# Sparse attention with a top-64 cut: GpSimd hides the found scores, VectorE counts the narrow tile, and the maxima move to the next step

## The reference

```python
q, k, v = split_heads(x @ Wq), split_heads(x @ Wk), split_heads(x @ Wv)   # x: 16 batches, 512 rows, 128 columns
k = concat([mem_k, k]); v = concat([mem_v, v])                # 16 memory keys before 512, 16 heads of 64
dots = einsum('bhid,bhjd->bhij', q, k) * 64 ** -0.5
dots = einsum('bhij,hk->bkij', dots, pre_proj)                # mix the heads
dots = where(causal, -FMAX, dots)
vk = top_k(dots, 64)[..., -1:]                                # each row's 64th largest score
dots = where(dots < vk, -FMAX, dots)
attn = einsum('bhij,hk->bkij', softmax(dots), post_proj)      # mix again
out = einsum('bhij,bhjd->bhid', attn, v) @ Wo + bo            # then a residual, layer norms and a gated FFN of 384
```

## Time and profile before

| | before |
|---|---|
| median of 3 runs | 3637.55 us (3636.05 to 3637.64) |
| the profiled execution | 3636.07 us, span 3634.3 us |
| VectorE busy | 3292.4 us, 91% |
| ScalarE busy | 3199.3 us, 88% |
| PE busy | 2795.9 us, 77% |
| GpSimd busy | 1551.4 us, 43% |

### The profile page before, as it was taken

How to read it: one execution, slowest core, us unless ns; L and a number is a source line. 1 busy time by engine, 2 the same in 40 slices (tenths; PEclk the granted TensorE clock), 3 DMA queues, 4 the chain that set the end, 5 groups by cost and what they waited for, 6 DMA issues and landing times. The chain is left out here.

```text
span 3634.3 us, 67348 instructions
## 1 busy us (share of the span) xinstructions
PE 2795.9 (77%) x13751; PEld 1808.7 (50%) x13751; DVE 3292.4 (91%) x12492; ACT 3199.3 (88%) x9018; POOL 1551.4 (43%) x2663
## 2 busy tenths in 40 slices
PE   7777778777777878778778867877777788877765
PEld 3455455545545545555455545544555455545544
DVE  4699999999999999999999999999999999999994
ACT  1799999999979999999999979998999999999973
POOL 3233444444434444444444444443444444444433
PEclk9888999988888899888998888899889998899886
DMA  1000000000000000000000000000000000000000
GB/s 41 7 2 2 5 8 5 8 2 5 8 4 8 5 8 2 5 8 5 8 5 7 2 4 8 5 8 2 5 8 5 8 5 8 2 5 8 2 7 4
DMA packets 31375, 22.37 MB, mean 6 GB/s; under 512 B 3201, under 2 KB 30338, under 8 KB 30722
## 3 DMA queue, kind: packets, MB, share of 16 engines
q1 hardware_dynamic: 30722, 16.03, 1.6%
HBM read 11.83 MB, written 4.19 MB: 4 GB/s over the span
## 5 line engine op out<-in xcount | busy, mean ns | idle before, releaser
L871 ACT ACTIVATE signs<-scores,state 128x528 int8<-128x528 f32 (+3 forms) x3072 | 1764.3, 574 | 181.8 <-DVE state L1149 103.4
L713 PE MATMUL s_bank<-xn,gT 128*128 128x512 f32 (+3 forms) x2048 | 900.6, 568 | 1.7 <-issue 0.7
L1269 POOL TENSOR_SCALAR probs<-probs,rinv 128x528 f32<-128x528 f32 (+3 forms) x1024 | 547.1, 553 | 507.3 <-DVE rinv L1053 507.3
L737 PE MATMUL t_bank<-ident,probs 128*128 128x128 f32 x2560 | 482.7, 313 | 299.1 <-POOL probs L1269 289.7
L724 PEld LDWEIGHTS y_bank<-u_all,probsT 128*128 128x128 f32 x5120 | 619.9, 194 | 133.4 <-issue 124.2
L724 PE MATMUL y_bank<-u_all,probsT 128*128 128x128 f32 x5120 | 625.2, 278 | 7.1 <-ACT probsT L882 7.1
L1260 POOL TENSOR_TENSOR offset<-consts,found 128x36 f32<-128x36 f32 x256 | 161.7, 632 | 1047.5 <-DVE work L1014 1047.5
L871 ACT ACTIVATION_READ_ACCUMULATOR signs<-scores,state 128x1 f32 x3072 | 575.7, 187 | 0.0
L737 PEld LDWEIGHTS t_bank<-ident,probs 128*128 128x128 f32 x2560 | 299.7, 153 | 506.8 <-issue 398.6
L1048 DVE SCALAR_TENSOR_TENSOR probs<-scores,kth,expo 128x528 f32<-128x528 f32 (+3 forms) x1024 | 522.8, 565 | 24.8 <-issue 19.1
L892 ACT ACTIVATE expo<-scores,negmax 128x528 f32<-128x528 f32 (+3 forms) x1024 | 535.0, 575 | 0.0
(11 more groups left out here) (148 smaller groups left out, 3384.9 us busy)
## 6 DMA issues: line engine op xcount, KB each, us to landing
xwork<-in_L_attn_x_dram SPq DMA_DIRECT2D x17, 256.0 KB, 2.8
xres<-in_L_attn_x_dram SPq DMA_DIRECT2D x16, 256.0 KB, 2.9
out_dram<-ybuf SPq DMA_DIRECT2D x16, 256.0 KB, 2.4
u_all<-in_L_attn_Wq_dram SPq DMA_DIRECT2D x1, 512.0 KB, 3.7
u_all<-in_L_attn_Wk_dram SPq DMA_DIRECT2D x1, 512.0 KB, 4.5
u_all<-in_L_attn_Wv_dram SPq DMA_DIRECT2D x1, 512.0 KB, 5.3
u_all<-in_L_attn_Wo_dram SPq DMA_DIRECT2D x1, 512.0 KB
expo<-in_L_ffn_w_gate_dram SPq DMA_DIRECT2D x1, 192.0 KB, 4.7
```

The source lines that it names most:

```text
L713: nc.tensor.matmul(score_part(t, 0, KEYS[t]), lhsT=gT[s % 2][:, t * P:(t + 1) * P], rhs=xn[par][:, 0:KEYS[t]], start=True, stop=False, ski ...
L737: mm = nc.tensor.transpose(t_bank[q % 2][:, at:at + P], probs[:, h % 2, KEY_AT[t] + j * P:KEY_AT[t] + (j + 1) * P], ident[:, :])
L871: nc.scalar.activation(signs[:, k, 0:ROW[t]], row(scores, ring(head_of(s, k + 1), RING), t), ACT.Sign, bias=guesses(s % STATES, k, GUESSES ...
L1269: nc.gpsimd.tensor_scalar(prb, prb, rinv[:, slot_p, t:t + 1], 1.0, ALU.mult, ALU.mult).then_inc(scaled, 1)
```

## The change

Four things are changed in a step.

1. The hiding leaves VectorE. POOL does `work = scores - work` in four instructions, one for each tile, after its scaling, and posts `hidden`. For a subtraction of 1 to hide a score, all scores are made tiny: a factor `UNIT = 2 ** -60` goes into `a_all` and `amem`, and is taken out again in the exponentials' scale and in `minus_unit`.
2. The maxima and the pick move from the end of a step to the beginning of the next one, and wait for `hidden`.
3. Of the four founds, two stay ahead of `probs` and two come behind `rinv`.
4. ScalarE counts three tiles for each guess, not four. The 144-wide tile is counted by VectorE (`marks`, `narrow`), three instructions a step, and one more small instruction merges them.

Beside these, POOL places the memory scores before it scales, PE makes all three turns before the flag's product, some of the extra products move by a step, and the FFN's and the last norm's VectorE and POOL work moves one step later. The number of transfers is the same.

```diff
-                        for p, t in enumerate(ORDER):
-                            at_least(act, counted[k], 4 * (g - k - 1) + p)
+                        for p, t in enumerate(ORDER[:3]):
+                            at_least(act, counted[k], 3 * (g - k - 1) + p)
                             nc.scalar.activation(signs[:, k, 0:ROW[t]], ...
...
+                    if applies:                                       # VectorE, first in the step
+                        dve.wait_ge(hidden, 4 * gp + 4)
+                        for p, t in enumerate(ORDER):
+                            v.max(candidates(past)[:, t, 1:9], work[:, AT[t]:AT[t] + ROW[t]]).then_inc(select_step, 1)
+                        dve.wait_ge(offset_ready, gp + 1)
...
                     if selects:
-                        count_found(ORDER[0])
-                        count_found(ORDER[1])
+                        for t in ORDER[:2]:
+                            count_found(t)
...
                         v.reciprocal(rinv[:, slot_p % 2, :], rowsum[:, :]).then_inc(rinv_ready, 1)
+                    if selects:
+                        for t in ORDER[2:]:
+                            count_found(t)
...
-                        v.scalar_tensor_tensor(out=work[:, :], in0=work[:, :], scalar=-FMAX,
-                                               in1=scores[:, bass.ds(slot_k, 1), :].squeeze(1),
-                                               op0=ALU.mult, op1=ALU.add).then_inc(select_step, 1)
...
+                        for k in counts_now:
+                            v.tensor_scalar(marks[:, k], row(scores, ring(head_of(s, k + 1), RING), 0),
+                                            guesses(now, k, GUESSES)[:, 0:1], None, ALU.is_ge, ALU.add,
+                                            accum_out=narrow[:, k:k + 1]).then_inc(narrow_step, 1)
...
+                        dve.wait_ge(narrow_step, len(counts_now))
+                        dve.sem_clear(narrow_step)
+                        v.scalar_tensor_tensor(out=narrow_miss, in0=narrow[:, :], scalar=-2.0, in1=narrow_aim,
+                                               op0=ALU.mult, op1=ALU.add).then_inc(guess_step, 1)
+                        v.tensor_tensor(wide_miss, wide_counts, wide_aim, ALU.subtract).then_inc(guess_step, 1)
...
+                        for p, t in enumerate(ORDER):                 # POOL, behind its scaling
+                            pool.wait_ge(found_ready, 4 * gk + p + 1)
+                            alone(pool)
+                            wrk = work[:, AT[t]:AT[t] + ROW[t]]
+                            nc.gpsimd.tensor_tensor(wrk, row(scores, slot_k, t), wrk, ALU.subtract).then_inc(hidden, 1)
```

More of the change, by code:

```diff
@@ L418, in build @@
         found_ready = sem("found_ready")
+        hidden = sem("hidden")
         offset_ready = sem("offset_ready")
+        narrow_step = sem("narrow_step")
         select_step = sem("select_step")
@@ L755, in step @@
                     if lagged(kind, s, LAG_P):
-                        turn(head_of(s, LAG_P), g - LAG_P, 0)
-                        turn(head_of(s, LAG_P), g - LAG_P, 1)
+                        for q in range(3):
+                            turn(head_of(s, LAG_P), g - LAG_P, q)
                     if flagged(kind, s):
@@ L1071, in step @@
                         norm_stats(kind, b, "X1", xres)
-                    if s == 14 and kind != "first":
+                    if 11 <= s < 11 + HC and kind != "first":
+                        c = s - 11
+                        dve.wait_ge(silu_pool, HC * (b - 1) + c + 1)
+                        v.scalar_tensor_tensor(out=f_up[:, c, :], in0=f_tanh[:, c, :], scalar=1.0,
+                                               in1=f_up[:, c, :], op0=ALU.add, op1=ALU.mult).then_inc(silu_ready, 1)
+                    if s == 15 and kind != "first":
@@ L1088, in top_scan @@
[L1088 to L1101, removed]
@@ L1255, in step @@
                         nc.gpsimd.tensor_copy(seed_place((s + 1) % STATES), seed[:, s, :, :]).then_inc(first_ready, 1)
-                    if lagged(kind, s, LAG_K):
-                        at_least(pool, kth_ready, g - LAG_K)
-                        pool.wait_ge(found_ready, 4 * (g - LAG_K) + 4)
-                        alone(pool)
-                        nc.gpsimd.tensor_tensor(offset[:, :, 0:9], ranks, found[:, :].unsqueeze(2).to_broadcast([P, T, 9]),
-                                                ALU.add).then_inc(offset_ready, 1)
-                    if lagged(kind, s, LAG_P):
-                        gp, slot_p = g - LAG_P, head_of(s, LAG_P) % 2
-                        pool.wait_ge(rinv_ready, gp + 1)
-                        at_least(pool, probs_ready, 4 * gp + 4)
-                        alone(pool)
-                        for t in SCORE_ORDER:
-                            prb = probs[:, slot_p, AT[t]:AT[t] + ROW[t]]
-                            nc.gpsimd.tensor_scalar(prb, prb, rinv[:, slot_p, t:t + 1], 1.0, ALU.mult,
-                                                    ALU.mult).then_inc(scaled, 1)
-                        if s == LAG_P and kind != "first":
-                            pool.wait_ge(misc_full, misc_index(kind, b, ("PM", 1)) + 1)
-                        pool.wait_ge(scaled, 4 * gp + 4)
-                        alone(pool)
-                        nc.gpsimd.tensor_copy(head_mem(pmem, head_of(s, LAG_P)), mem_parts(probs[:, slot_p, :])).then_inc(pmem_ready, 1)
                     if kind != "drain":
@@ L1286, in step @@
                                               head_mem(smem[par], s)).then_inc(mem_placed, 1)
+                    gp, slot_p = g - LAG_P, head_of(s, LAG_P) % 2
+                    if lagged(kind, s, LAG_P):
+                        pool.wait_ge(rinv_ready, gp + 1)
+                        at_least(pool, probs_ready, 4 * gp + 4)
+                        alone(pool)
+                        for t in SCORE_ORDER:
+                            prb = probs[:, slot_p, AT[t]:AT[t] + ROW[t]]
+                            nc.gpsimd.tensor_scalar(prb, prb, rinv[:, slot_p, t:t + 1], 1.0, ALU.mult,
+                                                    ALU.mult).then_inc(scaled, 1)
+                    if lagged(kind, s, LAG_K):
+                        gk, slot_k = g - LAG_K, ring(head_of(s, LAG_K), RING)
+                        for p, t in enumerate(ORDER):
+                            pool.wait_ge(found_ready, 4 * gk + p + 1)
+                            alone(pool)
+                            wrk = work[:, AT[t]:AT[t] + ROW[t]]
+                            nc.gpsimd.tensor_tensor(wrk, row(scores, slot_k, t), wrk, ALU.subtract).then_inc(hidden, 1)
+                        at_least(pool, kth_ready, gk)
+                        alone(pool)
+                        nc.gpsimd.tensor_tensor(offset[:, :, 0:9], ranks, found[:, :].unsqueeze(2).to_broadcast([P, T, 9]),
+                                                ALU.add).then_inc(offset_ready, 1)
+                    if lagged(kind, s, LAG_P):
+                        if s == LAG_P and kind != "first":
+                            pool.wait_ge(misc_full, misc_index(kind, b, ("PM", 1)) + 1)
+                        pool.wait_ge(scaled, 4 * gp + 4)
+                        alone(pool)
+                        nc.gpsimd.tensor_copy(head_mem(pmem, head_of(s, LAG_P)), mem_parts(probs[:, slot_p, :])).then_inc(pmem_ready, 1)
                     extras(kind, b, s)
```

150 lines of the change are left out of this document (79 added, 71 removed).

## The result

The change makes the kernel 8.8% slower: 3958.84 us median against 3637.6, ratio 1.0883 with a 95% interval of 1.0864 to 1.0902. The profiled execution's span is 3957.3 us, 323 more than before.

The account below looks back on a forecast made before the run. VectorE's list was taken as the bound. Hides holding its two-input instructions add 1.45 us a step: 256 x 1.45 = 371, + 12 = 383; 3636 + 383 = 4019, say 4020 us, 10.5% slower; range 3860 to 4120.

Parts of the forecast that it names:

- The bound: Whole kernel: VectorE's list sets the time, 12.29 us a plain step without gaps; ScalarE's time buys at most about 20 us.
- The split of the founds and the moved maxima cost the same as before: VectorE's step: these pieces only change places, and the flag's load stays between long instructions; no added time.
- VectorE's list with nothing held: VectorE's plain step after the change, if POOL held nothing: 11.78 us instead of 12.29.
- POOL's hides: POOL's four subtractions behind the scaling: 1.30, 1.02, 0.75 and 0.48 us, 3.55 in all, ending 6.04 us after rinv.
- The collision: After rinv, hides hold spread, missed and the merging instruction; update ends at 7.99 us, step 13.74 instead of 12.29, +1.45.
- The small POOL work: Offset, pmem and negmax on POOL behind the hides: counted as costing nothing, at most 0.7 us a step.
- The 12 us for the 48 steps: Steps s = 6, 7 and 14: spread was not held before, so 0.25 us isn't saved; 48 x 0.25 = 12 us.
- The sum: Whole run: 256 steps x 1.45 = 371, + 12 = 383 us more than 3636.
- the hides hold nothing: Rival: hides don't hold VectorE, so the chain rinv, scaling, hides, maxima, probs bounds at 11.9 us; 3548 us, chance 0.12.
- The narrow counts: Forecast: one-input counts run beside the hides. Rival: they are held too, step 14.75 us, 4278 us in all, chance 0.05.
- The hides' rate: POOL's hides: forecast 2.14 ns a column. Rival: a broadcast subtraction's 1.68 ns, step 13.27 us, 3899 us, chance 0.11.
- the sum hardly depends on the order: VectorE's small instructions beside the hides: whichever comes first, the update can't be over much before the hides are.

Follow-up runs that it names:

- Run 1: The changed kernel with POOL's four hides working on one column each and the maxima reading the unhidden scores: 3513.61 us, 0.9671 of before.
- run 5: The changed kernel with the narrow counts placed ahead of spread and missed: 3849.16 us, 1.0582 of before.
- run 2: The changed kernel with ScalarE counting all four tiles again, no narrow counts on VectorE: 3798.55 us, 1.0453 of before.
- run 7: The changed kernel with hiding back on VectorE, all counts on ScalarE, and the flag's load two founds later, behind the first found: 3675.12 us, 1.0101 of before.
- run 10: The changed kernel with hiding on VectorE, all counts on ScalarE, f_up early in the next step, flag's load behind the fourth maxima: 3510.77 us, 0.9658.
- run 6: The kernel before, with two of the four founds behind rinv, which also put the flag's load behind the first found: 3702.49 us, 1.0178 of before.

## Why the prediction was right

It forecast 4020 us in 3860 to 4120; 3958.8 was measured. By its steps:

- *The bound.* VectorE's list sets the time before and after; ScalarE's 378 us bought nothing. Right. But the step read as typical, 12.29 us, was not. It follows the memory maxima, and VectorE has no gap in it. The next step has one, between its last found and its first probs, 0.40 us from start to start instead of 0.28 (1487.37 to 1487.65 in the earlier trace rows):

```profile
1499.66 0.36 DVE L1014 TENSOR_SCALAR_CACHE_REDUCE work<-scores,state 128x144 f32<-128x144 f32 x1
...
1500.06 0.77 DVE L1048 SCALAR_TENSOR_TENSOR probs<-scores,kth,expo 128x528 f32<-128x528 f32 x1
```

  The gap is over 0.05 us in 170 steps. In the change, where the flag's load stands among the maxima, it is gone from the usual step. So "The split of the founds and the moved maxima cost the same as before" is wrong by 0.12 us a plain step, about 30 us of what the forecast was too high by.
- *VectorE's list with nothing held*, 11.78 us. Run 1 shows it: rinv to rinv is 11.76 us in its plain steps (median).
- *POOL's hides*: forecast 1.30, 1.02, 0.75, 0.48, measured 1.304, 1.029, 0.762, 0.489. They overlap a little, so that they end 5.91 us behind rinv, not 6.04. POOL is busy 470 us more, 1.84 a step, where the forecast has 3.6 - 1.2 = 2.4: it left out that the offset no longer waits either (671 ns before, 247 after).
- *The collision.* From the maxima to rinv 5.75 us, as forecast. From rinv to the maxima 7.80 instead of 7.99. The merging instruction comes at 5.75, not 5.96, since the founds follow rinv after 0.10 instead of 0.14, and missed is released at 4.7 instead of 4.8. It takes 171 ns, against 166 in run 1, and with the update behind it 2.05 us instead of 1.95. 0.19 x 256 = 49 us is the larger part of what was too much.
- *The small POOL work*, which the forecast let cost nothing. It costs: the update's next two instructions fall on the offset and the pmem copy. The first of them in the change, then in run 1:

```profile
L1152 DVE TENSOR_TENSOR state<-counts,consts x258: 153/283/1315, 115.1 to 3885.4; 128x9 f32<-128x9 f32 x129
...
L1152 DVE TENSOR_TENSOR state<-counts,consts x258: 152/160/174, 112.5 to 3440.3; 128x9 f32<-128x9 f32 x129
```

  The second (L1153) goes from 176 ns in run 1 to 267. (Before, the update has eleven instructions, not ten, from L1123 to L1149; in the change it has twelve from L1150 on.) From the merging instruction to the maxima it is 2.05 us in the change and 1.85 in run 1, so that 0.2 us a step is what it costs, within the 0.7 named as the most. The forecast's 1.95 with nothing held was 0.1 too long and covered half of it.
- *The 12 us for the 48 steps* in which spread was not held before: there. From start to start, spread takes 1.10 us more than before at s = 6, 7 and 14 and 0.80 on average in the others, 0.30 x 48 = 14 us. The other steps lost 31 us over the plain step's loss in all, 19 more than these 12; the forecast saw no difference there.
- *The sum.* Forecast 371 + 12 = 383 us; the spans differ by 323. The plain step is 79 us too high (292 instead of 371: 49 by the half step from rinv, 30 by the 12.29), the other steps 19 too low (31 instead of 12). The errors partly cancel, so the time is nearer than its terms.
- *The rivals.* That the hides hold nothing falls with run 1, which is the same list with hides of one column. The narrow counts are not held: 352 ns at the median with 362 at most, while they run beside the hides. The hides' rate is that of f_up and not of the broadcast subtraction.
- *The sentence that the sum hardly depends on the order* holds in the plain step (run 5) and not in the steps with one-input work to spare, where order is worth 2 us (16.07 against 13.96 at s = 6).

That the hides hold VectorE's two-input instructions is shown by run 1, and that one-input work beside them is not held by the counts and by L966 in run 2; which part of the two engines is shared is not seen in any run.

## What to carry to other kernels

Work moved from VectorE to GpSimd is not off VectorE's path if it is long and VectorE has small two-input instructions at that time: each of these can wait for the end of a whole GpSimd instruction (1.1 us here for four columns). Look in the trace for small instructions whose duration is that of the other engine's; then place GpSimd's long work beside VectorE's one-input work (founds, evictions, maxima, norm statistics), or shift VectorE's small instructions until GpSimd is done. And before one-input work is taken off VectorE, see whether it is not free where it stands. A step read as typical should be checked against the median of all steps: the one read here was 0.12 us short, 30 us over the run.

## What the runs showed of the hardware that had not been expected

A load of a flag into VectorE's registers with a branch behind it wants work of VectorE behind it. In run 7, 0.56 us between the two was too little: 0.33 us of idle time, and 0.20 from the accumulator's read to the next found, where 0 is usual, and 112 us a run. In the kernel before, where two founds (0.70 us) stand between, 0.12 us is lost in the usual step. With the rank instruction, the pick and two founds between (run 10), the time was 29 us better than with the load ahead of the third of the maxima.

From the start of the load to the start of the first probs behind the branch it takes 1.67 us at the median of runs 6 and 7 each, and 1.77 in the kernel before; in the kernels that have the load among the maxima or behind them it is over 2.5, and the gap is gone from the usual step. By these medians, an estimate is that VectorE needs about 1.7 us of work queued from the load's start on. In run 6, the step behind the memory maxima, which has longer work ahead of its founds, lost next to nothing; no run takes apart what the time goes to.
